# Transposes of the identity on TensorE and another order of ScalarE's steps in the first block of a Mamba-style mixer with an MLP

## The reference, cut to what matters

```python
x = L0_attn_hidden_states                      # (2, 1024, 512), float32
def mixer(h):                                  # 64 heads of 16, state 128, 4 taps
    proj = h @ W_in * mup_vector
    z, xBC, dt = split(proj, [1024, 1024 + 1280])
    xBC = silu(causal_conv(xBC, conv_w) + conv_b)
    x, B, C = xBC[..., :1024], xBC[..., 1024:1152], xBC[..., 1152:]
    dt = softplus(dt + dt_bias); dA = exp(-dt * exp(A_log))
    # for every token t and head:
    #   state = state * dA[t] + (dt[t] * x[t]) outer B[t];   y[t] = state @ C[t]
    g = (y + D * x) * silu(z)
    return (g * rsqrt(mean(g * g) + 1e-5) * norm_w) @ W_out
x = x + mixer(layernorm(x))
x = x + (silu((h := layernorm(x)) @ gate_w.T * gate_s) * (h @ up_w.T * up_s)) @ down_w.T * down_s
```

## Time and profile before

| | us |
|---|---|
| median of 3 timed runs | 775.84 |
| lowest and highest of them | 775.04, 778.64 |
| profiled execution, whole | 781.49 |
| its span, first to last instruction | 779.8 |
| busy in the span: PE / DVE / ACT / POOL | 742.3 / 520.5 / 492.4 / 293.4 |

### The profile page before, as it was taken

One profiled execution on the slowest core, in us unless ns is written; L12 is line 12 of the kernel. 1 busy time (PEld: TensorE's weight loads), 2 busy tenths in 40 slices (PEclk: granted clock), 3 DMA queues, 4 the chain that ended last, 5 costly groups with the idle time before them and its releaser, 6 DMA issues.

```text
span 779.8 us, 20312 instructions
## 1 busy us (share of the span) xinstructions
PE 742.3 (95%) x8486; PEld 609.8 (78%) x8486; DVE 520.5 (67%) x845; ACT 492.4 (63%) x933; POOL 293.4 (38%) x235
## 2 busy tenths in 40 slices
PE   4977999999999999999999998889999999999997
PEld 4855788888887887887887886568888888888886
DVE  6968976886887888797797796873633532632331
ACT  5989878978978977978879888533312321321330
POOL 2173275366456546627617707530010011001002
PEclk9988999999999999999999999999999999999999
DMA  9824243384485266266465378634113013003002
GB/s 297 228 69 109 44 105 111 92 241 127 82 236 142 79 158 211 88 148 201 139 158 184 83 202 316 200 99 160 41 55 108 0 37 125 0 13 95 0 1 84
DMA packets 42299, 94.97 MB, mean 122 GB/s; under 512 B 9888, under 2 KB 15776, under 8 KB 42016
## 3 DMA queue, kind: packets, MB, share of 16 engines
q1 hardware_dynamic: 42208, 93.67, 41.9%
HBM read 84.73 MB, written 17.57 MB: 131 GB/s over the span
## 4 chain that ended last, share of the span: by engine, by line
PE 60%; DVE 22%; ACT 10%; issue 5%; DMA 1%; POOL 1%; SPq 0%; DVEq 0%; ACTq 0%; POOLq 0%
PE ps_y L1684 10%; PE ps_proj L1671 9%; DVE cx L937 9%; PE ps_out L1671 6%; PE ps_x L1671 6%; PE ps_proj L1223 4%; PE ps_x L1272 4%; PE ps_proj L1224 3%; PE ps_proj L1225 3%; PE ps_y L1295 3%; DVE ring L992 3%; ACT ring L716 2%; DVE state L1002 2%; PE ps_x L1306 2%; DVE dt_p L912 2%
## 5 line engine op out<-in xcount | busy, mean ns | idle before, releaser
L531 POOL TENSOR_TENSOR ring<-tokd,ring 128x1024 f32<-128x1024 f32 x64 | 122.2, 1924 | 185.2 <-ACT tokd L711 127.5
L1223 PE MATMUL ps_proj<-xn_hi,win_x_hi 128*128 128x256 f32 x352 | 104.7, 298 | 1.7 <-DVE xn_lo L906 1.7
L1224 PE MATMUL ps_proj<-xn_lo,win_x_hi 128*128 128x256 f32 x352 | 100.2, 285 | 0.0
L1225 PE MATMUL ps_proj<-xn_hi,win_x_lo 128*128 128x256 f32 x352 | 100.0, 284 | 0.0
L937 DVE SCALAR_TENSOR_TENSOR cx<-cin,consts,cx 128x256 f32<-128x256 f32 x240 | 96.3, 475 | 0.0
L1540 POOL TENSOR_TENSOR res<-res,hidden 128x512 f32<-128x512 f32 (+1 forms) x16 | 20.1, 1256 | 166.3 <-DVE hidden L1603 165.3
L1223 PEld LDWEIGHTS ps_proj<-xn_hi,win_x_hi 128*128 128x128 f32 x352 | 67.7, 192 | 15.7 <-issue 14.0
L992 DVE TENSOR_TENSOR ring<-ring,ps_tok 128x1024 f32<-128x1024 f32 x64 | 75.6, 1214 | 4.8 <-ACT ring L720 4.7
L1223 PE MATMUL ps_proj<-xn_hi,win_z_hi 128*128 128x256 f32 x256 | 74.0, 289 | 0.0
L1224 PE MATMUL ps_proj<-xn_lo,win_z_hi 128*128 128x256 f32 x256 | 72.2, 282 | 0.0
L1225 PE MATMUL ps_proj<-xn_hi,win_z_lo 128*128 128x256 f32 x256 | 72.1, 282 | 0.0
(11 more groups left out here) (186 smaller groups left out, 1887.3 us busy)
## 6 DMA issues: line engine op xcount, KB each, us to landing
ring<-cum_dram SPq DMA_DIRECT2D x128, 256.0 KB, 4.8
xin<-x SPq DMA_DIRECT2D x8, 512.0 KB, 3.9
res<-x SPq DMA_DIRECT2D x32, 128.0 KB, 2.7
x_dram<-res SPq DMA_DIRECT2D x32, 128.0 KB, 2.9
res<-x_dram SPq DMA_DIRECT2D x16, 256.0 KB, 2.7
out<-res SPq DMA_DIRECT2D x15, 256.0 KB, 2.1
x_in_sb<-x_dram SPq DMA_DIRECT2D x3, 1024.0 KB, 5.6
gate_w_copy<-gate_w SPq DMA_DIRECT2D x4, 704.0 KB, 6.1
```

Of the source, the lines that this page charges most:

```text
L531: pool.tensor_tensor(ring[:, g, :, :], own, ring[:, g, :, :], ALU.subtract).then_inc(diffed, 1)
L1223: pe.matmul(out, hi[:, k, :], xn_hi[:, k, :], start=(k == 0), stop=False)
L1224: pe.matmul(out, hi[:, k, :], xn_lo[:, k, :], start=False, stop=False)
L1225: made = pe.matmul(out, lo[:, k, :], xn_hi[:, k, :], start=False, stop=(k == KT - 1))
```

## The change

TensorE gets a helper `keep_warm(n)`: n transposes of the 128 x 128 identity into `ps_out`, whose result nobody reads. It is called with 36 in front of the first `turn_xn` (after the wait for the identity, `filled`), with 10 behind the second, and in the first block with 16 between `turn_tok` and `turn_x` of step 0, with 12 in front of `group(0, 0)`, with 12 in front of `update(0, 1)`, and with 12 in front of `carry(0, 1)`.

ScalarE's order in step 0 of the first block changes: the copy of B (`keep_tok`), the first `clamp` and, behind it, the first `fade` with its table load stand ahead of `weight_hi(9)`, and each later `clamp` now stands directly ahead of its own `fade`. VectorE's `weight_lo(9)` moves behind the second `mix`. All other blocks keep their order.

```diff
@@ scalar, body @@
                 if not first:
                     evacuate(i, 6)
-                clamp(c, 0)
-                clamp(c, 1)
-                if not first:
+                if first:
+                    keep_tok(c)
+                    clamp(c, 0)
+                    fade(c, 0)
+                    clamp(c, 1)
+                else:
+                    clamp(c, 0)
+                    clamp(c, 1)
                     square(c - 1)
                     evacuate(i, 7)
-                keep_tok(c)
-                fade(c, 0)
-                clamp(c, 2)
+                    keep_tok(c)
+                    fade(c, 0)
+                    clamp(c, 2)
                 fade(c, 1)
+                if first:
+                    weight_hi(9)
+                    clamp(c, 2)
+                    fade(c, 2)
                 clamp(c, 3)
-                fade(c, 2)
+                if not first:
+                    fade(c, 2)
                 fade(c, 3)
@@ scalar, opening @@
             evacuate(0, 7)
-            weight_hi(9)
             body(0, True, False)
@@ vector, body @@
-                if first:
-                    weight_lo(9)
-                else:
+                if not first:
                     make_x1(c - 2)
                 mix(c, 0)
                 if not first:
                     scale_carry(i, 0)
-                for g in range(1, GROUPS):
-                    mix(c, g)
+                mix(c, 1)
+                if first:
+                    weight_lo(9)
+                mix(c, 2)
+                mix(c, 3)
@@ tensor @@
+            def keep_warm(n):
+                for _ in range(n):
+                    pe.transpose(ps_out[:, 0:P], eye[:], eye[:])
...
                 turn_tok(i, 0)
+                if first:
+                    keep_warm(16)
                 turn_x(i, 0)
...
                     add_carry(c)
+                else:
+                    keep_warm(12)
                 group(c, 0)
...
                     sum_squares(c - 1)
+                else:
+                    keep_warm(12)
                 update(c, 1)
...
                     project(i + 1, 2)
+                if first:
+                    keep_warm(12)
                 carry(i, 1)
...
             pe.wait_ge(filled, 1)
+            keep_warm(36)
             turn_xn(0, 0, True)
             turn_xn(0, 1, True)
+            keep_warm(10)
```

## The result

The changed kernel is slower: 780.8 us at the median of 22 runs, against 776.1 us for 22 runs of the kernel before on the same chip, ratio 1.0054 (95% interval 1.0036 to 1.0072). The forecast was 773.7 us, its range ended at 777.3. The profiled execution after has 781.28 us (span 779.6), that of before 781.49 (span 779.8). The prediction took the recorded execution's 5.65 us above the median as common to both kernels. It is not: before was recorded in one of its longest executions, after in an ordinary one. So the ratio has to come from the timed runs, and the two traces tell where time moves.

A forecast was written before the change was run, and what follows sets the result against it. From 79 us TensorE is the bound, so gains ahead of it reach the end. Chain 0.45 us plus carry 1.7 us, 2.15 us off the 775.84 us median, gives 773.7 us, range 770.5 to 777.3.

The forecast's parts named there:

- the sum: Total gain forecast at the end: 0.45 us from the first block's chain plus 1.7 us from the carry, 2.15 us.
- the clock not rising: Rival, 15%: transposes neither raise nor hold TensorE's clock, so project(0, 0) starts 1.7 us late; 777.1 us, at worst 778.8.
- Transposes and the clock: Claim that transposes count as work holding TensorE's clock up; no row of the trace was said to settle it.
- The opening: Block 0's first products run at full clock, project(0, 0) still starting at 12.0 us; ScalarE gains 1.55 us.
- The delay of the first product behind the 36 transposes: TensorE ahead of the first turn_xn: lateness from the added transposes, put at 0 (ends: 0 and 0.3 us).
- `evacuate(0, 1)` has no wait: Sign on ScalarE in the opening: its 1.15 us wait for project(0, 1) goes.
- GpSimd keeps the clamp waiting: ScalarE behind the copy of B: clamp(0, 0) waits for the first diff, a new wait of 0.55 us.
- the three pairs: ScalarE in block 0: each clamp directly ahead of its fade loses overlap, costing 0.6 us in all.
- The last `mix`: End of block 0's step 0 chain: starts at 50.4 instead of about 50.95; 0.45 us taken (ends: -0.3 and 1.0).
- The carry: carry(0, 1) on TensorE runs at full clock, 3.63 to 1.94 us; the whole 1.7 us arrives at the end.
- not in the timed runs: Rival, 20%: timed executions of before mostly had the fast carry(0, 1) already, so only 0.45 us is gained; 775.4 us.
- All slow time at half its length: Rival, 13%: TensorE is the bound throughout, so half of some 18 us of slow-clock time goes, 9 us; 766.8 us.

The follow-up runs named there:

- e4_block: The changed kernel with 30 more transposes, 256 added TensorE instructions in all; 777.28 us, ratio 1.0011 to the kernel before.
- e5_after_256: The changed kernel with 15 idle products between group(0, 0) and group(0, 1), 256 added instructions in all; ratio 0.9981 to the kernel before.
- e9_lo_first: e4_block with VectorE's norm_lo(1, 0) and norm_lo(1, 1) moved ahead of weight_lo(11); ratio 0.9997 to the kernel before.
- e12_256_lo_first: e5_after_256 with VectorE's norm_lo(1, 0) and norm_lo(1, 1) moved ahead of weight_lo(11); ratio 0.9997 to the kernel before.
- e1_order: The kernel before with only the new ScalarE and VectorE order, no transposes; 777.35 us, ratio 1.0001.
- e3_pad: The kernel before with 49 idle products in the opening, 196 added instructions, no transposes, old order; 783.16 us, ratio 1.0088.
- e6_pad_256: e3_pad with 15 more idle products between group(0, 0) and group(0, 1), 256 added instructions in all; ratio 0.9991 to the kernel before.
- e8_pad_128: The kernel before with 32 idle products in the opening, 128 added instructions; ratio 1.0067.
- e10_pad_64: The kernel before with 16 idle products in the opening, 64 added instructions; ratio 1.0079.
- e13_pad_80: The kernel before with 20 idle products in the opening, 80 added instructions; ratio 1.0021.
- e2_warm: The kernel before with only the 98 added transposes, ScalarE and VectorE in the old order; 780.93 us, ratio 1.0065.

## Why the prediction was wrong

- **The step that failed** is in its first paragraph: "a microsecond gained at 79 us on TensorE and on VectorE alike is a microsecond at the end, and the change touches nothing behind it". The diff touches no operation behind 79 us, but it moves every later instruction of TensorE by 196 places in the stream that is fetched. The four after-like kernels with 256 added (e4_block, e5_after_256, e9_lo_first, e12_256_lo_first) have a mean ratio of 0.9997, the changed kernel 1.0054: 0.0057 x 776 = 4.4 us that the sum had no term for. In the trace of after it is the pause of 2.22 us and 3.4 us at half clock behind it, 3.64 us lost between 76 and 112 us. The prediction gave the slower side to one rival (the clock not rising), and 4% to a time above 779.7; none of its cases held a cost in the later blocks.
- **Transposes and the clock**: right, and the rival by which they do nothing is refuted: the clock rose after transposes alone. The rule quoted there from the Trainium skill, "TensorE: Matmul & The Clock Gate", Part 4: PE-mode transpose, does not agree with this trace: the granted clock rose at 8.22 us, behind transposes alone.
- **The opening**: right in mechanism. The delay of the first product behind the 36 transposes, put at 0 to 0.3 us, is a term that no row shows; in the run there is none, the products start at 11.76 us instead of 11.99. `evacuate(0, 1)` has no wait, `evacuate(0, 2)` 0.26 us; GpSimd keeps the clamp waiting 0.32 us where 0.55 was said. From `evacuate(0, 7)` to `weight_hi(10)` ScalarE took 11.72 us, the 10.83 of before, this wait and 0.57 us, so the three pairs cost 0.57 where 0.6 was said. The last `mix` ends 1.18 us earlier, not 0.45; without the 0.5 us of the earlier weights it is 0.7.
- **The carry**: 3.63 to 1.94 us in the two recorded executions, exactly as said. But this is luck in part, and the rival "not in the timed runs" is largely right. Seven of the recorded kernels have none of the added transposes (before, e1_order, e3_pad, e6_pad_256, e8_pad_128, e10_pad_64, e13_pad_80). Their carry takes 1.94 us in four, 2.38 in e8_pad_128 and 3.63 and 3.68 in the other two. Those of e1_order and e6_pad_256:

```profile
74.82 1.94 PE L1282 MATMUL ps_x<-state,cx 128*64 128x512 f32 x8 [2.70 <-DVE xpad L987]
...
76.91 3.68 PE L1276 MATMUL ps_x<-state,cx 128*64 128x512 f32 x8 [4.12 <-DVE xpad L978]
```

By the mean of the seven, 2.49 us, the transposes are worth 0.55 us there and not 1.7 (an estimate from one execution each); with it the sum would have been 0.45 + 0.55 = 1.0 us. With the fetch's place restored the mean gain is 0.3 us, nearer to that than to 2.15. How much of the rest goes in collisions can't be told: each ratio is uncertain by 1.4 to 2.3 us.

- **All slow time at half its length**: refuted. From 0.989 to 0.998 of 775 us are 7 us by that working; the ratio of e9_lo_first says 0.2 us, and at most 2.6 us by its interval.
- **The profiled execution**: taking its 5.65 us above the median off both sides was wrong, since before's trace holds pauses at packet edges of its own (2.72 us at 484 us, 0.69 and 1.26 near 512) and after's holds others. It did not cause the miss.

## What to carry to other kernels

Code added to an engine's list can cost more than its own duration: it moves the places at which the next packet of instructions must have arrived, and in this kernel a row of very short instructions beside full DMA engines was a bad place. Before a small edit is judged, time it also with idle instructions that fill up one packet (here 256 for TensorE), and time the padding alone; if that moves the time as much as the edit, the edit has not been measured yet. And read the trace behind the last edited place too: look for waits ended by "issue" that the kernel before does not have. And a clock that was low in one recorded execution may be high in others: look at a second recording before a gain is counted on it.

## What the runs showed of the hardware

- **Instruction packets.** TensorE's stream comes in packets of 16384 bytes, 67 in this kernel and 68 with 256 instructions more; most take 0.9 to 1.9 us, the longest 3.4 (e13_pad_80). All 52 pauses over 0.4 us without a releaser in the 17 traces stand at a packet's edge (193 or 194 instructions past a multiple of 256) and end 1.1 to 1.65 us after a packet's landing. In all seven kernels with an edge inside `turn_tokd` of block 1, 2 or 3 in its first step, TensorE stood 1.7 to 3.8 us there, and a packet started within 1.1 us of the pause's beginning, before or after it. Between 80 and 480 us no other pause of these seven without a releaser is over 0.82 us. With less DMA traffic (share 0.2 to 0.7) the same routine paused 0.82 us at most.
- **The clock after such a pause.** After 2.22 us without work the clock went to 1.2 GHz for 3.4 us, which made the pause dearer than its length; so it did after 1.71 us in e2_warm and in four of the other five kernels, for 3.4 or 6.8 us. In e8_pad_128 it did not, after 2.08 us.
- **Transposes raise the clock.** In the changed kernel it rose at 8.22 us, when TensorE had done only transposes, from 2.10 us on.
- **VectorE and GpSimd side by side.** Two SCALAR_TENSOR_TENSOR of 128x512 took 3.04 us instead of 1.40 beside a GpSimd TENSOR_TENSOR of 128x1024, which took 2.39 us instead of 1.91; in e8_pad_128, where the `diff` had started 0.08 us before the two, they took 3.03 us and it kept its 1.90. VectorE's read from PSUM in the same place (`xn_lo`, 1.27 us in e9_lo_first, beside a `diff` of 1.90) was not slowed.
